# Sparsemax thresholds: three Newton rounds from another start in place of four, and the members compared row by row

## What is computed

```
scores = einsum('bhqd,bhkd->bhqk', qh, kh) * 32 ** -0.5      # 16 heads of 32
attn   = sparsemax(scores)                                   # over the 722 keys
x      = x + einsum('bhqk,bhkd->bhqd', attn, vh) @ Wo + bo
n      = layernorm(x)
x      = x + sqrt((n @ cos(theta + theta_noise)) ** 2 + (n @ sin(phi + phi_noise)) ** 2)
```

## Time and profile before

| what | value |
|---|---|
| runs shown | 681.27, 680.38 and 677.35 us, median 680.38 us |
| profiled execution | 676.18 us, its span 674.4 us |
| mean granted TensorE clock | 0.915 of full speed |
| VectorE busy | 573.3 us (85%) |
| TensorE busy | 571.3 us (85%) |
| ScalarE, GpSimd busy | 378.0 us (56%), 189.0 us (28%) |

### The profile page before, as it was taken

The page is one execution under the profiler, slowest core; times in us unless marked ns, Lnnn a source line. Parts: engine busy times, 40 slices in busy tenths (PEclk is TensorE's granted clock), DMA queues, the critical chain, the costliest instruction groups (busy, mean ns, idle before and its releaser), DMA issues.

```text
span 674.4 us, 14485 instructions
## 1 busy us (share of the span) xinstructions
PE 571.3 (85%) x4648; PEld 336.7 (50%) x4648; DVE 573.3 (85%) x2900; ACT 378.0 (56%) x657; POOL 189.0 (28%) x239
## 2 busy tenths in 40 slices
PE   2686999999913999899999999991899999988675
PEld 1343665656502655565556555651556565645431
DVE  5699999978967999999999999995999999999400
ACT  3674568767511667566756676661466666554321
POOL 2711322332220250435133422342024431310301
PEclk9968987999965999999999999996899999996768
DMA  9863022302230103130323022302203020300000
GB/s 309 273 173 91 16 63 74 96 7 62 84 84 0 31 11 98 55 98 5 85 69 105 0 61 89 103 11 61 76 9 98 20 54 27 80 7 9 13 1 12
DMA packets 33506, 44.25 MB, mean 66 GB/s; under 512 B 8386, under 2 KB 26818, under 8 KB 33415
## 3 DMA queue, kind: packets, MB, share of 16 engines
q1 hardware_dynamic: 32332, 41.16, 21.4%
q10 hardware_dynamic: 1088, 2.10, 0.9%
HBM read 23.77 MB, written 1.64 MB: 38 GB/s over the span
## 4 chain that ended last, share of the span: by engine, by line
PE 49%; DVE 26%; issue 11%; ACT 7%; SPq 4%; DMA 2%; POOL 1%; DVEq 0%; POOLq 0%; ACTq 0%
PE ring L463 29%; DVE cand L952 7%; PE mix_bank L583 3%; PE ring L612 3%; DVE dif L966 3%; PE ring L514 3%; PE ring L558 3%; DVE f_sum L975 3%; SPq L255 3%; DVE over L969 3%; ACT S L692 3%; PE ring L531 2%; DVE n_over L977 2%; DVE dif L970 2%; PE ring L501 1%
## 5 line engine op out<-in xcount | busy, mean ns | idle before, releaser
L952 DVE MAX8 cand<-S 100x8 f32<-100x45 f32 (+1 forms) x2048 | 223.5, 195 | 2.1 <-issue 0.4
L463 PE MATMUL ring<-wv,ctx 128*121 128x512 f16 x576 | 154.5, 390 | 0.0
L463 PE MATMUL ring<-ctx,wk 128*128 128x361 f16 x768 | 125.7, 323 | 4.7 <-DVE ctx L1118 4.7
L817 ACT ACTIVATE pT<-ring 121x800 f32<-121x800 f32 x96 | 80.5, 839 | 72.3 <-PE ring L612 71.6
L692 ACT ACTIVATE S<-ring 100x722 f32<-100x722 f32 x128 | 95.5, 773 | 32.6 <-PE ring L558 32.6
L463 PEld LDWEIGHTS ring<-ctx,wk 128*128 128x128 f16 x768 | 75.1, 99 | 50.0 <-issue 7.1
L340 POOL TENSOR_TENSOR ctx<-ctx_f,ctx 128x484 f16<-128x484 f32 x42 | 51.5, 1225 | 149.8 <-ACT ctx L692 149.4
L463 PEld LDWEIGHTS ring<-wv,ctx 128*121 128x121 f16 x576 | 71.4, 136 | 34.0 <-issue 7.7
L348 POOL TENSOR_TENSOR ks<-k_f,ks 128x361 f16<-128x361 f32 x64 | 57.9, 905 | 79.6 <-ACT k_f L704 76.7
L558 PE MATMUL ring<-kst,qst 96*100 96x361 f16 x256 | 65.1, 348 | 11.5 <-DMA kst<-ks 8.9
L612 PEld LDWEIGHTS ring<-qst,kst 99*121 99x121 f16 x768 | 59.3, 147 | 29.7 <-issue 13.8
(11 more groups left out here) (124 smaller groups left out, 722.9 us busy)
## 6 DMA issues: line engine op xcount, KB each, us to landing
kst<-ks SPq DMA_DIRECT2D x384, 45.1 KB, 1.9
ctx_f<-in_ctx SPq DMA_DIRECT2D x45, 242.0 KB, 2.9
xq<-in_x SPq DMA_DIRECT2D x8, 200.0 KB
xr<-in_x SPq DMA_DIRECT2D x8, 200.0 KB
out_y<-att SPq DMA_DIRECT2D x8, 200.0 KB
S<-in_L_xattn_Wk ACTq DMA_DIRECT2D x1, 1024.0 KB, 6.9
wq<-in_L_xattn_Wq ACTq DMA_DIRECT2D x1, 1024.0 KB, 11.4
wcos<-in_L_ffn_theta SPq DMA_DIRECT2D x1, 1024.0 KB, 10.4
```

Source lines behind the costliest of these rows:

```text
L463: last = nc.tensor.matmul(psum, lhs(c, i), w(c, j), start=(c == 0 and n == 0), stop=(c == DC - 1 and n == 2))
L817: nc.scalar.activation(pT[0:CK, u % 3, :, :], src, ACT.Relu).then_inc(two_read, 1)
L952: last = nc.vector.max(pieces[:, h, :, n], S[0:L, HH * (i % 2) + h, cuts[n]:cuts[n + 1]])
```

## The change

- There are three rounds, on 3, 6 and 7 ranks (`RANKS`), in place of four on 2, 4, 6 and 7.
- The start is 0.9 times the old one plus 0.1 times the row's maximum `top`. The steps behind the first two rounds are stretched by 1.0 and 1.12; behind a stretched one tau is capped at `top`.
- Marks and clipped differences lie in one float32 tile `dif` of two halves and are summed by one reduction into `sums` (`f_sum` and `n_over` are its halves). `fold` is gone. A mark that is 0 becomes 2^-32, so that no count is 0.
- The last step may also be negative, since the clamp at 0 is gone.
- Behind the comparison with the final tau, VectorE counts the members in the first seven ranks (`n_still`) and compares this with the last round's count (`changed`, 0 or 1 in each row). `flag_ready` rises only then.
- TensorE sums `changed` and the marks of rank 8, and no longer those of ranks 1 to 7. Whatever has a sum over 0.5 is refined as before. `read_flags`, `settle`, `refine` and `split_again` are the same text.

```diff
--- before.py
+++ after.py
@@ -25,10 +25,11 @@
 LN_EPS = 1e-5
 SUM_TOL = 1e-5
 PIECES = 16
-RANKS = (2, 4, 6, 7)
-STRETCH = (1.15, 1.1, 1.0, 1.0)
+RANKS = (3, 6, 7)
+STRETCH = (1.0, 1.12)
+TOWARDS_MAX = 0.1
 ROUNDS_MORE = 14
-TINY = 2.0 ** -20
+TINY = 2.0 ** -32
 SCRATCH = 2048
 
 
@@ -149,12 +150,15 @@
         sq = sb("sq", [L, 2, D])
         q_f, x2n = sq[:, 0, :], sq[:, 1, :]
         cand = sb("cand", [L, HH, NCAND])
-        dif, over = sb("dif", [L, HH, PIECES * max(RANKS)]), sb("over", [L, HH, NCAND], BF16)
-        fold = sb("fold", [L, HH, 2 + PIECES * max(RANKS) // 2], BF16)
+        dif = sb("dif", [L, 2, HH, PIECES * max(RANKS)])
+        over = dif[:, 1, :, :].bitcast(BF16)[:, :, 0:NCAND]
         tau = sb("tau", [L, 2, HH])
-        f_sum, step_t, n_over = (sb(n, [L, HH]) for n in ("f_sum", "step_t", "n_over"))
+        sums = sb("sums", [L, 2, HH])
+        f_sum, n_over = sums[:, 0, :], sums[:, 1, :]
+        step_t, top = sb("step_t", [L, HH]), sb("top", [L, HH])
         zero = sb("zero", [L, 1])
-        one_b, minus_b = sb("one_b", [L, 1], BF16), sb("minus_b", [L, 1], BF16)
+        n_still, changed = sb("n_still", [L, HH]), sb("changed", [L, HH])
+        one_b = sb("one_b", [L, 1], BF16)
         bit_c, code, lost = (sb(n, [1, HH]) for n in ("bit_c", "code", "lost"))
         word_i = sb("word_i", [1, 1], I32)
         again, againT = sb("again", [P, 32]), sb("againT", [P, 32])
@@ -539,11 +543,9 @@
                 pe.wait_ge(flag_ready, i + 1)
                 if i > 0:
                     pe.wait_ge(aT_ready, 2 * i)
-                nc.tensor.matmul(flag_ps[:, :, PIECES], ones[:, :], n_over[:, :], start=True, stop=True)
-                for r in range(8):
-                    last = nc.tensor.matmul(flag_ps[:, :, 0:PIECES], (one_b if r == 7 else minus_b)[:, :],
-                                            marks[:, :, r, :], start=(r == 0), stop=(r == 7))
-                last.then_inc(flag_sum, 1)
+                nc.tensor.matmul(flag_ps[:, :, PIECES], ones[:, :], changed[:, :], start=True, stop=True)
+                nc.tensor.matmul(flag_ps[:, :, 0:PIECES], one_b[:, :], marks[:, :, 7, :], start=True,
+                                 stop=True).then_inc(flag_sum, 1)
 
             def scores(i, heads):
                 b, part = divmod(i, 2)
@@ -957,36 +959,40 @@
                 t = tau[:, i % 2, :]
                 t3 = t.rearrange("p (g a) -> p g a", a=1)
                 after(found)
-                n = counted(nc.vector.tensor_reduce(f_sum[:, :], cand[:, :, 0:PIECES], AX, ALU.add))
+                counted(nc.vector.tensor_reduce(top[:, :], cand[:, :, 0:PIECES], AX, ALU.max))
+                n = counted(nc.vector.tensor_reduce(f_sum, cand[:, :, 0:PIECES], AX, ALU.add))
                 after(n)
-                n = counted(nc.vector.tensor_scalar(t, f_sum[:, :], -1.0, 1.0 / PIECES, ALU.add, ALU.mult))
+                n = counted(nc.vector.tensor_scalar(t, f_sum, -1.0, (1.0 - TOWARDS_MAX) / PIECES, ALU.add, ALU.mult))
+                after(n)
+                n = counted(nc.vector.scalar_tensor_tensor(t, top[:, :], TOWARDS_MAX, t, ALU.mult, ALU.add))
                 for turn, ranks in enumerate(RANKS):
                     E = PIECES * ranks
+                    above, member = dif[:, 0, :, 0:E], dif[:, 1, :, 0:E]
                     after(n)
-                    n = counted(nc.vector.tensor_tensor(dif[:, :, 0:E], cand[:, :, 0:E],
-                                                        t3.broadcast_to([L, HH, E]), ALU.subtract))
+                    n = counted(nc.vector.tensor_tensor(above, cand[:, :, 0:E], t3.broadcast_to([L, HH, E]), ALU.subtract))
                     after(n)
-                    n_mask = counted(nc.vector.tensor_scalar(over[:, :, 0:E], dif[:, :, 0:E], 0.0, None, ALU.is_ge))
-                    n_dif = counted(nc.vector.tensor_scalar(dif[:, :, 0:E], dif[:, :, 0:E], 0.0, None, ALU.max))
-                    after(n_mask)
-                    n_fold = counted(nc.vector.tensor_tensor(fold[:, :, 2:2 + E // 2], over[:, :, 0:E // 2],
-                                                             over[:, :, E // 2:E], ALU.add))
-                    after(n_dif)
-                    counted(nc.vector.reduce_sum(f_sum[:, :], dif[:, :, 0:E], AX))
-                    after(n_fold)
-                    n_count = counted(nc.vector.reduce_sum(n_over[:, :], fold[:, :, 0:2 + E // 2], AX))
-                    after(n_count)
-                    n = counted(nc.vector.reciprocal(step_t[:, :], n_over[:, :]))
+                    counted(nc.vector.tensor_scalar(member, above, 0.0, TINY, ALU.is_ge, ALU.max))
+                    n = counted(nc.vector.tensor_scalar(above, above, 0.0, None, ALU.max))
                     after(n)
-                    n = counted(nc.vector.scalar_tensor_tensor(step_t[:, :], f_sum[:, :], -1.0, step_t[:, :],
+                    n = counted(nc.vector.reduce_sum(sums[:, :, :], dif[:, :, :, 0:E], AX))
+                    after(n)
+                    n = counted(nc.vector.reciprocal(step_t[:, :], n_over))
+                    after(n)
+                    n = counted(nc.vector.scalar_tensor_tensor(step_t[:, :], f_sum, -1.0, step_t[:, :],
                                                                ALU.add, ALU.mult))
                     after(n)
                     if turn < len(RANKS) - 1:
                         n = counted(nc.vector.scalar_tensor_tensor(t, step_t[:, :], STRETCH[turn], t, ALU.mult, ALU.add))
-                nc.vector.scalar_tensor_tensor(t, step_t[:, :], 0.0, t, ALU.max, ALU.add).then_inc(tau_ready, 1)
+                    if turn < len(RANKS) - 1 and STRETCH[turn] > 1.0:
+                        after(n)
+                        n = counted(nc.vector.tensor_tensor(t, t, top[:, :], ALU.min))
+                nc.vector.tensor_tensor(t, step_t[:, :], t, ALU.add).then_inc(tau_ready, 1)
                 dve.wait_ge(tau_ready, i + 1)
-                nc.vector.tensor_tensor(over[:, :, :], cand[:, :, :], t3.broadcast_to([L, HH, NCAND]),
-                                        ALU.is_ge).then_inc(flag_ready, 1)
+                n = counted(nc.vector.tensor_tensor(over[:, :, :], cand[:, :, :], t3.broadcast_to([L, HH, NCAND]), ALU.is_ge))
+                after(n)
+                n = counted(nc.vector.reduce_sum(n_still[:, :], over[:, :, 0:PIECES * max(RANKS)], AX))
+                after(n)
+                nc.vector.tensor_tensor(changed[:, :], n_still[:, :], n_over, ALU.not_equal).then_inc(flag_ready, 1)
 
             def two_steps(t):
 
```

More of the change, by code:

```diff
@@ L167, in build_kernel @@
         st2, mv2, sd2 = sb("st2", [L, 6]), sb("mv2", [L, 2]), sb("sd2", [L, 2])
-        relu_row = dif[:, :, :].rearrange("p g n -> p (g n)")[:, 0:N]
-        mask_row = over[:, :, :].rearrange("p g n -> p (g n)")[:, 0:N]
+        relu_row = dif[:, :, :, :].rearrange("p a g n -> p (a g n)")[:, 0:N]
+        mask_row = dif[:, 1, :, :].rearrange("p g n -> p (g n)").bitcast(BF16)[:, 0:N]
         marks = over[:, :, :].rearrange("p g (r n) -> p g r n", r=8)
@@ L1130, in _ @@
             nc.vector.memset(one_b[:, :], 1.0).then_inc(dve_const, 1)
-            nc.vector.memset(minus_b[:, :], -1.0).then_inc(dve_const, 1)
             for h in range(HH):
                 counted(nc.vector.memset(bit_c[:, h:h + 1], 2.0 ** h))
-            n = [counted(nc.vector.memset(again[:, :], 0.0)), counted(nc.vector.memset(zero[:, :], 0.0)),
-                 counted(nc.vector.memset(fold[:, :, 0:2], TINY))][-1]
+            n = [counted(nc.vector.memset(again[:, :], 0.0)), counted(nc.vector.memset(zero[:, :], 0.0))][-1]
             after(n)
```

## The result

The changed kernel takes 1980.46 us (median of 4 runs, 1979.14 to 1981.35) against 679.2 us, 2.9155 times the time before (95% interval 2.9055 to 2.9255). The prediction was 1994 us, with 1870 to 2150 as its range.

The account below looks back on a forecast made before the run. VectorE was taken as the bound, with nothing beside a refinement; 674.4 - 43.2 (old refinements) - 8 (thresholds) + 1365 (120 refined heads) = 1988 us, plus 1.8 around the span and 4.2 to the median: 1994 us, range 1870 to 2150.

Parts of the forecast that it names:

- The number of heads: Formulas of both kernels on the reference's scores: 120 of 128 heads flagged for refinement by 367 rows, against three before.
- Its reason: Why 367 rows are flagged: the count is compared one Newton round earlier; the row-by-row comparison is not the source.
- No cover for a refinement: TensorE and VectorE have nothing beside a refinement; the old kernel's three refined heads cost 43.2 us together.
- The terms of the 1365 us: Cost of refining 120 heads: bodies 1021, gaps 260, skipped heads 5, entries 20, exits with split and TensorE's release 59 us.
- the gaps: VectorE's time between the refinement bodies of neighbouring heads: 2.5 us each, 104 of them, 260 us.
- the entries: Idle time from VectorE's last maximum to a set's first refinement: 1.27 us each, sixteen of them, 20 us.
- the exits: Time from a set's last refined head to the split: 2.5 us in each of sixteen sets.
- The bodies: VectorE's refinement of one head, from L1029 to the end of L1020: 8.51 us each, 120 of them, 1021 us.
- Prices for branches against the rows: Gap by the skill's branch prices: 0.5 us, sum some 210 us less; the rows' longer gaps were taken.
- The thresholds: VectorE's rounds save 2.2 to 2.6 us a set, the verdict adds 1.8; net 0.5 a set, 8 us faster.
- TensorE after a stop: After a refinement TensorE's 29 us to its flag sums end about with VectorE's work; VectorE stays the bound by 1 or 2 us.
- The rival of three refinements: Heads settle as before, only three are refined and the kernel is faster, 672 us; chance 3%.

Follow-up runs that it names:

- the signed verdict: Changed kernel, but each row gives TensorE the signed difference of last round's and final count, in place of 0 or 1 for unequal: 623.72 us, ratio 0.9182.

## Why the prediction was right, point by point

- **The number of heads.** 120 were worked out, and 120 ran. This was the step that carried everything. It was safe because the same arithmetic gave the three refinements of the trace before, at their places. That it came out to the very head has some luck in it: in three of the experiments it was one head short, each time behind set 2. By the formulas other rows flag that head (head 2) in the changed kernel anyway.
- **Its reason was wrong.** "The old count was taken before the fourth step, the new one before the third, so one Newton round fewer has to have found the final members" tells half. That a fourth round cures it is shown (744.95 us), and with the stretches exchanged three rounds leave 49 rows whose counts fall. But the prediction also said that the row-by-row comparison "is not where the 367 come from", and the signed verdict shows that it matters: with signs no head is flagged. Three rounds with that stretch leave 367 rows unsettled, and the inequality is what notices them. I had worked out how many rows change and not in which direction. It changed nothing in the time, but someone who had gone by my sentence would have looked for the cause in the wrong instruction.
- **No cover for a refinement.** Right: without them the kernel before is 40.6 us faster, and TensorE's waits in front of L602 are 1340.9 us.
- **The terms of the 1365 us.** In sum 1356.7 were measured, as the difference of the runs with and without; the agreement has opposite errors in it. By the idle times before L1035 the gaps were 236.9/104 = 2.28 us (2.5 assumed), the entries 45.6/16 = 2.85 (1.27 assumed, from the only one that had head 0 flagged), and the exits 23.2/16 = 1.45 (2.5 assumed), with 1.16 for the split and the release of TensorE (1126.73 to 1127.89; 1.17 assumed). The bodies took 8.74 us on average (8.49 to 10.55), where 8.51 was taken. These terms add up to 1373 us, 16 more than the difference of the two runs. The entries were the term with the largest error for its size: 1.27 us was the shorter of the two in the trace before, the other was 4.47.
- **Prices for branches against the rows.** The rows were the better guide for the whole gap: by the estimate of 0.5 us a gap that the prediction worked out from the figures in the Trainium skill, the sum would have been some 200 us too low. A gap is mostly not branches: in the one of 1.89 us the load of the verdict (L1040) alone has a record of 0.32 us.
- **The thresholds.** 8 us less were forecast, 13.5 measured (637.23 against 623.72), but not where the prediction put them. It put all 8 on VectorE's thresholds, which became 2.9 us shorter, and costed TensorE's flag sums at nothing, which no run here confirms: more than half of the saving lies outside VectorE's thresholds. Beside 1357 us this did not matter.
- **TensorE after a stop.** It did not become the bound. Its first scores came 16.1 us after the release (1127.89 to 1143.95), its flag sums 23.8 us after it (1151.71). VectorE's comparison of that set starts at 1147.30, and its verdict is out some 2.6 us later, at 1149.9; TensorE comes 1.8 us behind it, but VectorE reads the sums only behind the maxima of four heads, 7 us. That margin was enough. The granted clock fell further than before, to 0.54, but over the 23.8 us to the flag sums it was 0.90 again. VectorE's last instructions of two sets lie 118.7 us apart on average, where some 115 were forecast.
- **The rival of three refinements** is out, and the distance tells how far: break-even was one head more.

## What to carry to other kernels

- Where a branch at run time repairs what a fast path leaves, the time hangs on how often it is taken. Work that out from the data with the formulas of both versions, and first make the arithmetic reproduce the count in the trace before. Then look also at the sign and the size of what is left over.
- Saving a step of an iteration makes its verdict fire for everything that the saved step would have settled. With 100 rows to a flag, 3% of the rows flag 94% of the heads.
- A stretched step wants a verdict that sees a rising count. An unclamped last step with a test for inequality seems to fire on rounding as well: behind set 2, which needed no refinement before, both kernels here that ran four rounds with this verdict refined a head, where the formulas have a candidate at 0.00000003 from tau. That rounding is the cause was not tested.

## What the runs showed of the hardware

Some of VectorE's operations with one input tensor take about 0.8 us longer than others on as many elements. In one set of the changed kernel all three such cases have a GpSimd instruction beside them, as VectorE and GpSimd by time show:

```profile
1009.92 1.20 POOL L344 TENSOR_TENSOR ctx<-ctx_f,ctx 128x484 f16<-128x484 f32 x1 [89.16 <-ACT ctx L694]
...
1010.22 1.12 DVE L974 TENSOR_SCALAR dif<-dif 100x384 f32<-100x384 f32 x1
...
1011.26 0.35 DVE L975 TENSOR_SCALAR dif<-dif 100x384 f32<-100x384 f32 x1
...
1014.67 1.09 POOL L344 TENSOR_TENSOR ctx<-ctx_f,ctx 128x484 f16<-128x484 f32 x1 [3.55 <-ACT ctx L694]
1014.74 1.43 DVE L975 TENSOR_SCALAR dif<-dif 100x768 f32<-100x768 f32 x1
...
1019.40 1.46 POOL L344 TENSOR_TENSOR ctx<-ctx_f,ctx 128x484 f16<-128x484 f32 x1 [3.65 <-ACT ctx L694]
...
1019.96 1.38 DVE L974 TENSOR_SCALAR dif<-dif 100x896 f32<-100x896 f32 x1
...
1021.26 0.61 DVE L975 TENSOR_SCALAR dif<-dif 100x896 f32<-100x896 f32 x1
```

L974 on 384 elements takes 1.12 us with GpSimd's L344 beside it, where L975 on as many takes 0.35 free of it. L975 on 768 takes 1.43 us, L974 on 896 1.38, where L975 on 896 takes 0.61. Each of the three starts within GpSimd's instruction and ends 0.2 to 0.5 us behind its end: 1010.22 to 1011.34 against 1011.12, 1014.74 to 1016.17 against 1015.76, 1019.96 to 1021.34 against 1020.86.

Over the whole trace L974 and L975 ran 96 times, and 12 of them are long. Each of the 12 began within a GpSimd instruction. Of the others all but one began outside of one, and they kept their length even where GpSimd began while they ran; the one (L975 at 763.56) began 0.01 us behind GpSimd's. The reduction L977 began within a GpSimd instruction eight times and never took longer for it (1.75 us on 1536 elements, 2.02 on 1792).

The Trainium skill, "GPSIMD Engine Reference", section Specifications, says that GpSimd shares its interfaces to SBUF with VectorE, and that VectorE's instructions contend with it when they are in a two-port mode or have two inputs in SBUF. The trace does not name an instruction's mode, but what it shows fits: L974 and L975 pass 896 elements in 0.61 us, while L977, which is not touched, takes 2.02 for twice as many, 1.01 for each 896. No run here moved GpSimd's work away to show it as the cause.
